# The bias of V passed through Wo once, in place of a bias matmul in every V product

## The chip, the core and the metric

One Trainium2 chip; the program runs on one of its cores. The time is device microseconds (us) of one execution, and each kernel's figure is the median of its runs. Names of engines: PE is the matrix engine (TensorE), DVE VectorE, ACT ScalarE, POOL GpSimd, and SP the engine whose queue issues the DMAs here (SyncE).

## The reference

A gated block for eight batch items of 512 rows by 512 columns: cross attention with 16 heads of 32 columns, and then a feed-forward part with ternary weights. Cut to what the change touches:

```python
V = _linear(value, Wv, bv)                 # value @ Wv.T + bv, value is ctx_1024, 512 x 512 for each item
attn = jax.nn.softmax(qk / (2.0 * t), axis=-1)
out = jnp.einsum('bhqk,bhkd->bhqd', attn, V)
out = out.transpose(0, 2, 1, 3).reshape(b, sq, d)
return _linear(out, Wo, bo)                # out @ Wo.T + bo
...
x = x + jnp.tanh(g_xattn[0]) * _L0_xattn_ref(_layernorm(x), ctx_1024, ctx_1024, ...)
x = x + jnp.tanh(g_ffn[0]) * _L0_ffn_ref(_layernorm(x), w1, w2)
```

The rows of `attn` sum to one, so the bias `bv` reaches `out` unchanged in every row, and Wo turns it into one vector that is the same for all items: `Wo @ bv`. That vector and `bo` are added to the same result. What is computed besides: a temperature t for each head, from statistics of the scores and of their softmax (stage A below), a layer norm of x ahead of Q, and a quantisation of the activations in the feed-forward part.

## The kernel before

**Products.** Every f32 operand of Q, K, V and Wo is split into two f16 parts, high and low. One product of a 128x512 tile is twelve matmuls (four chunks of the contraction, and for each high x high, high x low, low x high), summed in one PSUM bank, by `split_product`. A bias is a thirteenth matmul: ones (128x128) times `bias16`, a tile that is zero except for two rows, the high and the low part of the bias (L1432 in `split_product`). K and Q get their biases on ACT as they leave PSUM; V and the Wo product (called W) get them by the thirteenth matmul.

**Stages.** `body(i)` runs on each engine for i = -1, 0, then three turns of a loop of two bodies for i = 1 to 6, then 7 and 8. In one body three things are interleaved: stage A of item i (64 score tiles, each a matmul L1455, a row maximum on DVE L998, an exponential on ACT L778, statistics on DVE L1008), stage B of item i-1 (its real attention, then W, the residual, the norm and the feed-forward part), and stage P of item i+1 (products K, V, Q, and the turned x). For i = -1 there is only P of the first item, for i = 0 no B, for 7 no P.

**Order within a body**, the same on all engines and written out by hand: 16 sets of stage B with 40 of the 64 A tiles among them; then the products K0 to K3, W0 to W3, the turned x, V0 to V2, Q0, Q1, the four transposes of the quantised residual (`turned_xq`, L1592), Q2, Q3, with the remaining A tiles spread over them by `A_PLAN`; then the feed-forward part (`up`, `turn`, `down`), and V3 after `up(1)`. Each engine runs its instructions in program order and waits on semaphores. Four PSUM banks (b_ps twice, o_ps, z_ps) are used in turn for all products (`mm_use`, `take`, by the list of uses in `bank_uses`); `take` makes PE wait until the bank's last user has drained it. In i = 0, eight chunks of the feed-forward weights are made ternary besides: their magnitudes are summed first (ACT L768 and DVE L1290), and chunk 7 is the last to be loaded.

**The first item's setup.** SP issues all loads in one row: Wk, ctx, x, Wq, then the small vectors (`bq` and `bk` laid out with one element for each partition and group, L561 and L562; the gates L563 and L564; `bv` and `bo` as rows copied to all partitions, L565 and L566), Wv, Wo, the small weights and three feed-forward chunks; then `stack` (the K and Q parts laid out for the scores, L493, L480, L487, 12 DMAs each), which waits for the splits of K and Q on POOL (L684). ACT runs a tanh of the two gates (L752) ahead of its first product drain (L847 and L851).

Of the kernel before, what the change touches and what calls it, by code (L numbers as in the profile page):

```python
# [72 lines left out]
BIAS_STEPS = 5  # L73
# [6 lines left out]
FIRST_V_AT = {1: 2, 3: 3}  # L80
POOL_CHUNKS, DVE_CHUNKS = (3, 2), (0, 1, 6, 7, 4, 5)
# [48 lines left out]
def bank_uses(setup, has_p, has_b, has_a):  # L130

    def some(stage, count, present=True):
        return [(stage, k) for k in range(count)] if present else []

    uses = some("S", 2, setup == 0) + some("K", C, has_p) + some("W", T, has_b)
    if setup == 0:
        uses += some("V", T, has_p) + some("X", T, has_p)
    else:
        uses += some("X", T, has_p) + some("V", T - 1, has_p and setup is None)
    uses += some("Q", C, has_p)[:2] + some("xq", T, has_b and has_p) + some("Q", C, has_p)[2:]  # L140
    uses += some("V", T, has_p and setup == -1)
# [82 lines left out]
def flamingo_kernel(nc, x, ctxT, g_xattn, g_ffn, WqT, bq, WkT, bk, WvT, bv, WoT, bo,  # L224
                    w1T, b1, w2T, b2, w3T, b3, f1T, f2T, out):
    with ExitStack() as ctx:
# [59 lines left out]
        bias16 = sb("bias16", [P, 2, D], F16)  # L286
        bias_row = vbuf[0][:, 0:2, :]
        bias_hi = vbuf[0][:, 2, :].bitcast(F16).rearrange("p (k n) -> p k n", k=2)
# [70 lines left out]
        bias_in, bias_step = sem("bias_in"), sem("bias_step")  # L359
# [76 lines left out]
        def _(sp):  # L436
# [149 lines left out]
        def _(pool):  # L586
# [21 lines left out]
            pool.memset(bias16[:, :, :], 0.0).then_inc(bias_step, 1)  # L608
# [67 lines left out]
            def body(i, par):  # L676
# [30 lines left out]
                for n in range(C):  # L707
                    if has_p:
                        split_qk(n)
                    if second and n % 2 == 1:  # L710
                        normalise_x(1, n // 2, from_cin)
                        split_x(1, n - 1, from_cin)
                        split_x(1, n, from_cin)
                    if has_b and n == 1:
                        split_y(i - 1, C - 1)
                if second:
                    make_ternary(3)
# [257 lines left out]
        def _(dve):  # L975
# [281 lines left out]
            def make_ternary(n):  # L1257
# [17 lines left out]
            vec.tensor_copy(bias16[0:1, :, :], bias_hi[0:1, :, :]).then_inc(bias_step, 1)  # L1275
            vec.scalar_tensor_tensor(out=bias16[DK:DK + 1, :, :], in0=bias_row[DK:DK + 1, :, :], scalar=WSCALE,
                                     in1=bias_hi[DK:DK + 1, :, :], op0=ALU.mult, op1=ALU.subtract) \
                .then_inc(bias_step, 1)
            weight_lo(2, "v")
# [13 lines left out]
            def body(i, par):  # L1293
                has_a, has_b, has_p = stages(i)
                second = isinstance(i, int) and i == 0
                for s in range(SETS):
# [5 lines left out]
                    if has_p and has_b and s in X_STATS_AT:  # L1302
                        stat_x(i + 1, X_STATS_AT.index(s))
                    if second and s in SUMS_AT:
                        ternary_sum(SUMS_AT[s])
# [97 lines left out]
        def _(pe):  # L1403
# [14 lines left out]
            def split_product(bank_n, left, right, tiles=(), bias=None):  # L1418
# [7 lines left out]
                for n, (c, l, r) in enumerate(pairs):  # L1426
                    if n in places:
                        places[n]()
                    ins = mat(mm_ps[bank_n][:, :], left[l](c), right[r](c),  # L1429
                              start=(c, l, r) == pairs[0], stop=bias is None and (c, l, r) == pairs[-1])  # L1430
                if bias is not None:
                    ins = mat(mm_ps[bank_n][:, :], ones16[:, :], bias16[:, bias, :], start=False, stop=True)  # L1432
# [56 lines left out]
            def body(i, par):  # L1489
# [41 lines left out]
                def w_part(t, chunks):  # L1531
# [5 lines left out]
                    if chunks[-1] == C - 1:  # L1537
                        mat(mm_ps[bank_n][:, :], ones16[:, :], bias16[:, 1, :], start=False, stop=True) \
# [18 lines left out]
                for t in range(T) if has_p or not has_b else ():  # L1557
                    if has_b:
                        split_product(take(i, "W", t),
                                      [lambda c, l=l: yT[:, l, c, t * P:(t + 1) * P] for l in range(2)],  # L1560
                                      [lambda c, w=w: w["o"][:, c, :] for w in (w_hi, w_lo)], tiles_a(C + t), bias=1)
# [12 lines left out]
                def v_products(tiles_of=range(T)):  # L1574
                    for t in tiles_of:
# [37 lines left out]
                for n in range(C):  # L1613
# [7 lines left out]
                    if first and n == C - 1:  # L1621
                        pe_waits.wait_ge(w_lo_done, 3)
                        pe_waits.wait_ge(bias_step, BIAS_STEPS)
                        v_products()
                    if has_b and has_p and n == 1:
# [139 lines left out]
```

## Time and profile before

| | |
|---|---|
| median of three runs | 1337.31 us (1337.2 to 1338.84) |
| the profiled execution, its own time | 1338.21 us |
| its span in the trace | 1336.3 us |
| PE busy | 89% |
| DVE busy | 82% |
| ACT busy | 70% |
| granted clock of PE, mean over the span | 0.967 |

Busy time is the sum of an engine's instructions; for PE their ends are modelled and the instructions overlap, so a busy PE is not one at its peak. The chain of work that ended last is followed back from the last instruction, at each step to what released it. Where two releasers are nearly as late as each other, it names only one of them. Times of rows are counted from the start of the span.

### The profile page before, as it was taken

To read this page: it belongs to the slowest core of one execution; us is meant where nothing else is said; L and a number is where in the kernel's file an instruction comes from. 1 tells how busy PE (TensorE), PEld (TensorE's weight loads), DVE (VectorE), ACT (ScalarE), POOL (GpSimd) and SP (SyncE) were. 2 spreads that over 40 slices of the span, in tenths; PEclk is the share of its full clock that TensorE was granted. 3 is DMA by queue.
4 is the path that set the end of the run, shared out by engine and by line. 5 is a ranking of instruction groups with operands and counts; after the bars stand their busy time and mean duration, and the time that the engine had idled before them with its cause. 6 is when DMAs were issued, how large, how long until landed. Compare 5 with 4: busy or idle time off the path is not lost.

```text
span 1336.3 us, 23530 instructions
## 1 busy us (share of the span) xinstructions
PE 1183.3 (89%) x6684; PEld 438.0 (33%) x6684; DVE 1097.7 (82%) x2054; ACT 936.5 (70%) x1568; POOL 394.2 (29%) x387
## 2 busy tenths in 40 slices
PE   4856598989999999998999999998989899859988
PEld 2322221444124421444124432344214441224234
DVE  7789789896998869896998869897898979985256
ACT  4676599565985679575985669665885669765833
POOL 3148555311452024510353124510353101200120
PEclk9878789999999999999999999999999999979989
DMA  8712211221112221211112221112212210001000
GB/s 311 233 58 64 48 48 49 48 48 57 33 41 48 57 74 49 48 36 39 54 49 48 51 79 48 25 25 65 64 49 49 48 65 1 1 1 42 23 0 32
DMA packets 36049, 73.70 MB, mean 55 GB/s; under 512 B 8144, under 2 KB 8528, under 8 KB 35408
## 3 DMA queue, kind: packets, MB, share of 16 engines
q1 hardware_dynamic: 35920, 72.13, 18.9%
q8 instruction: 62, 1.02, 0.3%
q14 instruction: 67, 0.55, 0.1%
HBM read 38.39 MB, written 8.39 MB: 35 GB/s over the span
## 4 chain that ended last, share of the span: by engine, by line
PE 50%; DVE 26%; issue 10%; ACT 8%; SPq 3%; DMA 1%; DVEq 1%; POOL 1%; ACTq 0%; POOLq 0%
PE b_ps L1429 10%; DVE stat L1008 7%; PE o_ps L1669 6%; DVE nmax L998 5%; PE o_ps L1474 4%; PE o_ps L1429 4%; PE b_ps L1461 4%; ACT region L810 4%; PE a_ps L1455 4%; PE z_ps L1429 4%; ACT etile L778 3%; DVE hmax L1204 2%; PE z_ps L1669 2%; PE z_ps L1485 2%; PE b_ps L1634 2%
## 5 line engine op out<-in xcount | busy, mean ns | idle before, releaser
L778 ACT ACTIVATE etile<-a_ps,nmax 128x512 f32<-128x512 f32 x512 | 368.0, 732 | 113.8 <-DVE nmax L998 113.5
L810 ACT ACTIVATE region<-b_ps,inv2t 128x512 f32<-128x512 f32 x512 | 353.2, 754 | 49.9 <-PE b_ps L1461 45.8
L998 DVE TENSOR_REDUCE nmax<-a_ps 128x1 f32<-128x512 f32 x512 | 345.5, 677 | 51.7 <-PE a_ps L1455 48.1
L1008 DVE BATCH_NORM_STATS2 stat<-etile 128x6 f32<-128x512 f32 x500 | 339.8, 682 | 16.0 <-ACT etile L778 15.7
L1455 PE MATMUL a_ps<-kst,qst 96*128 96x512 f16 x512 | 198.8, 392 | 32.9 <-ACT etile L778 26.7
L1461 PE MATMUL b_ps<-qst,kst 97*128 97x512 f16 x512 | 193.0, 389 | 22.4 <-DVE region L1230 7.8
L1474 PE MATMUL o_ps<-region,vbuf 128*32 128x512 f32 x1024 | 137.3, 608 | 10.7 <-ACT region L810 7.0
L1485 PE MATMUL z_ps<-region,ones 128*32 128x512 f32 x1024 | 136.2, 604 | 9.5 <-DVE region L1040 9.5
L1461 PEld LDWEIGHTS b_ps<-qst,kst 97*128 97x128 f16 x512 | 49.3, 96 | 288.9 <-ACT region L810 258.1
L684 POOL TENSOR_TENSOR region<-region 128x512 f16<-128x512 f32 x64 | 77.0, 1203 | 210.9 <-ACT region L851 210.9
L640 POOL TENSOR_TENSOR region<-region 128x512 f32<-128x512 f32 x32 | 40.8, 1276 | 288.9 <-DVE region L1047 288.9
L1204 DVE TENSOR_REDUCE hmax<-region 128x1 f32<-128x512 f32 x128 | 82.1, 680 | 13.2 <-ACT region L931 12.1
L613 POOL CAST c_hi<-cin 128x512 f16<-128x512 f32 x28 | 17.1, 610 | 243.8 <-DMA cin<-in_ctxT_dram 243.3
L1669 PE MATMUL o_ps<-f,region 128*128 128x512 fp8e4 x352 | 79.6, 379 | 0.0
L1455 PEld LDWEIGHTS a_ps<-kst,qst 96*128 96x128 f16 x512 | 50.9, 99 | 82.4 <-ACT etile L778 45.3
L1634 PE MATMUL b_ps<-f,region 128*128 128x512 fp8e4 x256 | 62.9, 383 | 14.2 <-DVE region L1230 11.5
L931 ACT ACTIVATE region<-b_ps,xmax 128x512 f32<-128x512 f32 x64 | 43.4, 689 | 26.3 <-PE b_ps L1634 26.0
L661 POOL TENSOR_SCALAR cin<-cin,mv,rstd 128x512 f32<-128x512 f32 x28 | 58.0, 2077 | 2.8 <-POOL rstd L652 2.6
L941 ACT ACTIVATE region<-b_ps 128x1024 f16<-128x1024 f16 x31 | 31.7, 1023 | 31.8 <-PE b_ps L1645 31.0
L1037 DVE TENSOR_SCALAR region<-o_ps 128x512 f32<-128x512 f32 x32 | 21.7, 680 | 37.0 <-PE o_ps L1474 37.0
L650 POOL TENSOR_SCALAR rstd<-mv 128x2 f32<-128x2 f32 (+1 forms) x25 | 5.8, 231 | 137.6 <-DVE mv L1353 52.4
L1669 PEld LDWEIGHTS o_ps<-f,region 128*128 128x128 f16 x352 | 33.7, 98 | 38.1 <-issue 1.0
(312 smaller groups left out, 1977.8 us busy)
## 6 DMA issues: line engine op xcount, KB each, us to landing
kst<-region SPq DMA_DIRECT2D x96, 128.0 KB, 2.3
qst<-region SPq DMA_DIRECT2D x84, 128.0 KB, 2.3
xres<-in_x_dram SPq DMA_DIRECT2D x8, 1024.0 KB, 5.5
out_dram<-xres SPq DMA_DIRECT2D x32, 256.0 KB, 2.0
cin<-in_ctxT_dram SPq DMA_DIRECT2D x30, 256.0 KB, 2.7
cin<-in_x_dram SPq DMA_DIRECT2D x28, 256.0 KB, 2.6
kst<-in_f1T_dram SPq DMA_DIRECT2D x2, 1024.0 KB, 9.4
qst<-in_f2T_dram SPq DMA_DIRECT2D x2, 1024.0 KB, 9.0
```

Source lines behind the costliest of these rows:

```text
L778: nc.scalar.activation(etile[:, k % E_SLOTS, :], a_ps[k % A_BANKS][:, :], ACT.Exp, bias=nmax[:, slot_of(n), t:t + 1], scale=1.0, accum_out ...
L810: nc.scalar.activation(probs[:, (s + 1) % 2, g, :], b_ps[g % 2][:, :], ACT.Exp, scale=inv2t[:, slot:slot + 1]).then_inc(b_exp, 1)
L998: vec.tensor_reduce(nmax[:, slot_of(k // T), k % T:k % T + 1], a_ps[k % A_BANKS][:, :], AX.X, ALU.max, negate=True).then_inc(a_max, 1)
L1008: vec.bn_stats(stat[:, slot_of(k // T) * T + k % T, :], etile[:, k % E_SLOTS, :]).then_inc(a_stat, covered)
L1204: ins = vec.tensor_reduce(hmax[:, n:n + 1], hbuf[t % 2][:, n * S:(n + 1) * S], AX.X, ALU.max, apply_absolute_value=True)
L1429: ins = mat(mm_ps[bank_n][:, :], left[l](c), right[r](c), start=(c, l, r) == pairs[0], stop=bias is None and (c, l, r) == pairs[-1])
L1455: mat(a_ps[k % A_BANKS][:, :], qst[par][0:SHIFT, slot, t * P:(t + 1) * P], kst[par][0:SHIFT, slot, :], start=True, stop=True).then_inc(a_f ...
L1461: mat(b_ps[g % 2][:, :], kst[par][0:SHIFT + 1, slot, k * P:(k + 1) * P], qst[par][0:SHIFT + 1, slot, :], start=True, stop=True).then_inc(b ...
L1474: ins = mat(o_ps[g * DK:(g + 1) * DK, :], vbuf[par][:, k, n * DK:(n + 1) * DK], probs[:, (s + 1) % 2, g, :], start=k == 0, stop=k == T - 1)
L1485: ins = mat(z_ps[g * DK:(g + 1) * DK, :], ones32[:, 0:DK], probs[:, (s + 1) % 2, g, :], start=k == 0, stop=k == T - 1)
L1634: ins = mat(mm_ps[bank_n][:, :], xqT[:, c, t * P:(t + 1) * P], f1[:, c, n * S:(n + 1) * S], start=c == 0, stop=c == C - 1)
L1669: ins = mat(mm_ps[bank_n][:, :], hT[t % 2][:, k, :], f2[:, k, :], start=k == 0, stop=k == KC - 1)
```

## The change

The thirteenth matmul of the V products is left out. In the setup of the first item `Wo @ bv` is computed once: SP loads `bv` into `bvc` with one element for each partition and chunk (as `bq` is loaded); POOL splits it into two f16 parts and spreads each over 64 columns (`spread_bv`); PE runs a product of twelve matmuls and the bias matmul of `bo`, 64 partitions wide, as a new use "O" of a PSUM bank behind V3 (`bias_product`); DVE takes it from PSUM behind set 13 of i = 0 and writes its high and low parts into `bias16` (`join_biases`), which now has one bias in place of two.

```diff
+BIAS_AT = 13
@@ bank_uses
-    uses += some("V", T, has_p and setup == -1)
+    uses += some("V", T, has_p and setup == -1) + some("O", 1, setup == -1)
@@ SP, setup
                 sp.dma_start(bqk[:, 1, :], bk.rearrange("(g p) -> p g", p=P)).then_inc(bqk_in, 16)
+                sp.dma_start(bvc[:, :], bv.rearrange("(g p) -> p g", p=P)).then_inc(bias_in, 16)
             sp.dma_start(gates[:, 0:1], g_xattn.partition_broadcast(P)).then_inc(gate_in, 16)
             sp.dma_start(gates[:, 1:2], g_ffn.partition_broadcast(P)).then_inc(gate_in, 16)
-            sp.dma_start(bias_row[:, 0, :], bv.partition_broadcast(P)).then_inc(bias_in, 16)
-            sp.dma_start(bias_row[:, 1, :], bo.partition_broadcast(P)).then_inc(bias_in, 16)
+            sp.dma_start(bias_row, bo.partition_broadcast(P)).then_inc(bias_in, 16)
@@ POOL; called in body(-1) behind the splits of K
+            def spread_bv():
+                pool_waits.wait_ge(bias_in, 32)
+                pool.tensor_copy(bv_parts[:, 0, :], bvc[:, :]).then_inc(bv_step, 1)
+                pool_waits.wait_ge(bv_step, 1)
+                pool.tensor_tensor(bv_parts[:, 1, :], bvc[:, :], bv_parts[:, 0, :], ALU.subtract).then_inc(bv_step, 1)
+                pool_waits.wait_ge(bv_step, 2)
+                pool.tensor_copy(bv_wide[:, :, :], bv_parts[:, :, :].rearrange("p l c -> p (l c)").unsqueeze(2)
+                                 .broadcast_to([P, 2 * C, HALF])).then_inc(bv_step, 1)
@@ DVE; called in body(0) behind set 13
+            def join_biases():
+                bank_n, before = mm_use(-1, "O")
+                dve_waits.wait_ge(mm_full[bank_n], before + 1)
+                vec.tensor_copy(bias_sum[0:HALF, :], mm_ps[bank_n][0:HALF, :]).then_inc(bias_step, 1)
+                dve_waits.wait_ge(bias_step, BIAS_STEPS + 1)
+                vec.tensor_copy(bias16[0:1, :], bias_sum[0:1, :]).then_inc(bias_step, 1)
+                vec.tensor_tensor(bias16[DK:DK + 1, :], mm_ps[bank_n][DK:DK + 1, :], bias_sum[DK:DK + 1, :],
+                                  ALU.subtract).then_inc(mm_free[bank_n], 1)
@@ PE, v_products
-                                          tiles_a(C + T + t) if t < T - 1 or not has_b else (), bias=0)
+                                          tiles_a(C + T + t) if t < T - 1 or not has_b else ())
@@ PE; called in body(-1) behind v_products
+                def bias_product():
+                    bank_n = take(i, "O")
+                    pe_waits.wait_ge(bv_step, 3)
+                    pe_waits.wait_ge(w_lo_done, 4)
+                    for n, (c, l, r) in enumerate((c, l, r) for c in range(C) for l, r in ((0, 0), (0, 1), (1, 0))):
+                        mat(mm_ps[bank_n][0:HALF, :], bv_wide[:, l * C + c, :], (w_hi, w_lo)[r]["o"][:, c, :],
+                            start=n == 0, stop=False)
+                    mat(mm_ps[bank_n][0:HALF, :], ones16[:, 0:HALF], bias16[:, :], start=False, stop=True) \
+                        .then_inc(mm_full[bank_n], 1)
```

What this moves in the engines' orders, at three places. On PE, at the end of the first item's setup, the last three matmuls of V3 (wv, c) are followed by the bias matmul and then by the A tiles of i = 0 (kst, qst). Before:

```order
L1429 MATMUL b_ps<-wv_hi,c_hi 128x512
L1429 MATMUL b_ps<-wv_lo,c_hi 128x512
L1429 MATMUL b_ps<-wv_hi,c_lo 128x512
L1432 MATMUL b_ps<-bias,ones 128x512
L1455 MATMUL a_ps<-kst,qst 128x512 x8
```

And in the changed kernel:

```order
L1460 MATMUL b_ps<-wv_hi,c_lo 128x512
L1624 MATMUL b_ps<-wo_hi,bv_wide 64x512
L1624 MATMUL b_ps<-wo_lo,bv_wide 64x512
L1624 MATMUL b_ps<-wo_hi,bv_wide 64x512 x2
L1624 MATMUL b_ps<-wo_lo,bv_wide 64x512
L1624 MATMUL b_ps<-wo_hi,bv_wide 64x512 x2
L1624 MATMUL b_ps<-wo_lo,bv_wide 64x512
L1624 MATMUL b_ps<-wo_hi,bv_wide 64x512 x2
L1624 MATMUL b_ps<-wo_lo,bv_wide 64x512
L1624 MATMUL b_ps<-wo_hi,bv_wide 64x512
L1626 MATMUL b_ps<-bias,ones 64x512
L1486 MATMUL a_ps<-kst,qst 128x512 x8
```

The bias matmul of V3 is gone, and thirteen narrower ones stand ahead of the A tiles (the first two pairs of A tiles stand ahead of V2 and V3 in both kernels).

On DVE, in i = 0, the row maximum and the statistics of set 13 are followed by those of set 14. In the changed kernel:

```order
L1016 TENSOR_REDUCE nmax<-a_ps 128x1
L1026 BN_STATS stat<-etile 128x6
L1302 CAST bv_wide<-b_ps 64x512
L1304 COPY bias<-bv_wide 1x512
L1305 TENSOR_TENSOR bias<-b_ps,bv_wide 1x512
L1016 TENSOR_REDUCE nmax<-a_ps 128x1
L1026 BN_STATS stat<-etile 128x6
L1260 TENSOR_REDUCE wsum<-wabs 128x1
```

The three rows in the middle are new; the rows around them stand next to each other in the kernel before (as L998, L1008 and L1242).

On SP, in the setup, the small vectors stood before the change as

```order
L562 DMA bqk<-in_bk_dram 128x4x1
L563 DMA gates<-in_g_xattn_dram 128x1
L564 DMA gates<-in_g_ffn_dram 128x1
L565 DMA vbuf<-in_bv_dram 128x512
L566 DMA vbuf<-in_bo_dram 128x512
L551 DMA xres<-in_WvT_dram 128x4x512
```

and stand now as

```order
L567 DMA bqk<-in_bk_dram 128x4x1
L568 DMA bvc<-in_bv_dram 128x4x1
L569 DMA gates<-in_g_xattn_dram 128x1
L570 DMA gates<-in_g_ffn_dram 128x1
L571 DMA vbuf<-in_bo_dram 128x512
L556 DMA xres<-in_WvT_dram 128x4x512
```

The load of bv has moved ahead of the two gates and has the form of the loads of bq and bk.

## Rows read from the trace of the kernel before

**Rows 1.** The page: busy time (share) of two engines, and the chain by engine.
```profile
PE 1183.3 (89%) x6684; PEld 438.0 (33%) x6684; DVE 1097.7 (82%) x2054; ACT 936.5 (70%) x1568; POOL 394.2 (29%) x387
...
PE 50%; DVE 26%; issue 10%; ACT 8%; SPq 3%; DMA 1%; DVEq 1%; POOL 1%; ACTq 0%; POOLq 0%
```

**Rows 2.** The chain in time, at V0 of i = 1: start us, us, what.
```profile
260.36 2.59 PE b_ps L1429 x12
262.96 0.22 PE b_ps L1432
263.17 0.22 PE a_ps L1455
```

**Rows 3.** Waits over the whole span: us in total, times, longest us.
```profile
PEld b_ps L1592 <- ACT region L851: 6.2, 6, 1.0
```

**Rows 4.** Timeline of i = 1 around Q1, ACT, then PE: start us, us, [idle before <- releaser].
```profile
273.53 0.69 ACT L778 ACTIVATE etile<-a_ps,nmax 128x512 f32<-128x512 f32 x1 [0.50 <-DVE nmax L998]
...
275.35 1.27 ACT L778 ACTIVATE etile<-a_ps,nmax 128x512 f32<-128x512 f32 x2
276.52 0.69 ACT L847 ACTIVATE region<-b_ps,bqk 128x512 f32<-128x512 f32 x1
...
277.93 0.40 PE L1592 MATMUL b_ps<-ident,region 128*128 128x128 f16 x4 [0.86 <-ACT region L851]
```

**Rows 5.** Windows: length, busy us (x instructions) of each engine, PE clock, DMA share.
```profile
262.50:277.90 15.40, 13.84 (x73) 6.32 (x70) 15.14 (x29) 9.36 (x19) 1.16 (x1) 1.00 0.01 2
...
74.60:129.40 54.80, 39.90 (x156) 14.78 (x156) 54.69 (x82) 37.76 (x53) 33.73 (x27) 0.84 0.19 48
```

**Rows 6.** Timeline of PE in i = 1, from the end of V3 on.
```profile
294.05 0.38 PE L1432 MATMUL z_ps<-bias,ones 128*128 128x512 f16 x1
294.61 1.07 PE L1645 MATMUL b_ps<-ident,region 128*128 128x128 f16 x16 [0.18 <-DVE region L1221]
```

**Rows 7.** Timeline of SP's DMA issues in the setup.
```profile
6.73 4.23 SPq L563 DMA_DIRECT2D gates<-in_g_xattn_dram  x1
...
22.33 1.59 SPq L474 DMA_DIRECT2D kst<-ones  x1
30.08 8.45 SPq L493 DMA_DIRECT2D kst<-region  x12
...
48.76 7.60 SPq L487 DMA_DIRECT2D qst<-region  x12
...
58.63 1.07 SPq L514 DMA_DIRECT2D region<-in_f2T_dram  x1
```

**Rows 8.** Timeline of the setup: ACT's tanh of the gates, POOL's splits of K and Q.
```profile
18.17 0.20 ACT L752 ACTIVATE tg<-gates 128x2 f32<-128x2 f32 x1 [1.76 <-DMA gates<-in_g_ffn_dram]
...
22.40 1.54 POOL L684 TENSOR_TENSOR region<-region 128x512 f16<-128x512 f32 x1 [0.82 <-ACT region L851]
24.99 1.31 POOL L684 TENSOR_TENSOR region<-region 128x512 f16<-128x512 f32 x1 [1.05 <-ACT region L851]
27.58 2.48 POOL L684 TENSOR_TENSOR region<-region 128x512 f16<-128x512 f32 x1 [1.28 <-ACT region L851]
37.22 1.20 POOL L684 TENSOR_TENSOR region<-region 128x512 f16<-128x512 f32 x1 [7.17 <-ACT region L851]
```

**Rows 9.** Timeline of i = 0's first sets: PE, ACT, DVE.
```profile
55.34 1.05 PE L1455 MATMUL a_ps<-kst,qst 96*128 96x512 f16 x3
...
70.10 1.91 ACT L768 ACTIVATE f<-region 128x2048 f32<-128x2048 f32 x1 [2.81 <-DMA region<-in_f2T_dram]
...
72.71 0.69 DVE L1008 BATCH_NORM_STATS2 stat<-etile 128x6 f32<-128x512 f32 x1 [2.50 <-ACT etile L778]
...
74.60 2.65 DVE L1262 SCALAR_TENSOR_TENSOR f<-kst,whalf,f 128x2048 fp8e4<-128x2048 f32 x1 [1.14 <-ACT f L759]
```

**Rows 10.** Nearest operations to the join's three: page (us, mean ns), then timeline.
```profile
L1037 DVE TENSOR_SCALAR region<-o_ps 128x512 f32<-128x512 f32 x32 | 21.7, 680 | 37.0 <-PE o_ps L1474 37.0
...
30.71 0.41 DVE L1275 COPY bias<-vbuf 1x1024 f16<-1x1024 f16 x1
```

More of the change, by code:

```diff
@@ L72 @@
 LOWEST = -3.0e38
-BIAS_STEPS = 5
+BIAS_STEPS, HALF = 5, 64
 SETUP_STEPS = G4 + 6
@@ L285, in flamingo_kernel @@
         ones16 = sb("ones16", [P, P], F16)
-        bias16 = sb("bias16", [P, 2, D], F16)
-        bias_row = vbuf[0][:, 0:2, :]
-        bias_hi = vbuf[0][:, 2, :].bitcast(F16).rearrange("p (k n) -> p k n", k=2)
+        bias16 = sb("bias16", [P, D], F16)
+        bv_wide = sb("bv_wide", [P, 2 * C, HALF], F16)
+        bv_parts = sb("bv_parts", [P, 2, C], F16)
+        bvc = sb("bvc", [P, C])
+        bias_row = vbuf[0][:, 0, :]
+        bias_hi = vbuf[0][:, 2, :].bitcast(F16)[:, 0:D]
+        bias_sum = bv_wide[:, :, :].rearrange("p k n -> p (k n)")
         bqk = sb("bqk", [P, 2, C])
@@ L358, in flamingo_kernel @@
         bq_scaled = sem("bq_scaled")
-        bias_in, bias_step = sem("bias_in"), sem("bias_step")
+        bias_in, bias_step, bv_step = sem("bias_in"), sem("bias_step"), sem("bv_step")
         mm_full = [sem(f"mm_full{n}") for n in range(MM)]
@@ L607, in _ @@
             pool.memset(ones16[:, :], 1.0).then_inc(bias_step, 1)
-            pool.memset(bias16[:, :, :], 0.0).then_inc(bias_step, 1)
+            pool.memset(bias16[:, :], 0.0).then_inc(bias_step, 1)
+            def spread_bv():
[6 more added lines that the diff above has]
+                                 .broadcast_to([P, 2 * C, HALF])).then_inc(bv_step, 1)
             def split_c(b, c):
@@ L715, in body @@
                         split_y(i - 1, C - 1)
+                if first:
+                    spread_bv()
                 if second:
@@ L1274, in _ @@
             dve_waits.wait_ge(bias_step, 3)
-            vec.tensor_copy(bias16[0:1, :, :], bias_hi[0:1, :, :]).then_inc(bias_step, 1)
-            vec.scalar_tensor_tensor(out=bias16[DK:DK + 1, :, :], in0=bias_row[DK:DK + 1, :, :], scalar=WSCALE,
-                                     in1=bias_hi[DK:DK + 1, :, :], op0=ALU.mult, op1=ALU.subtract) \
+            vec.tensor_copy(bias16[0:1, :], bias_hi[0:1, :]).then_inc(bias_step, 1)
+            vec.scalar_tensor_tensor(out=bias16[DK:DK + 1, :], in0=bias_row[DK:DK + 1, :], scalar=WSCALE,
+                                     in1=bias_hi[DK:DK + 1, :], op0=ALU.mult, op1=ALU.subtract) \
                 .then_inc(bias_step, 1)
+            def join_biases():
[6 more added lines that the diff above has]
+                                  ALU.subtract).then_inc(mm_free[bank_n], 1)
             weight_lo(2, "v")
@@ L1303, in body @@
                         stat_x(i + 1, X_STATS_AT.index(s))
+                    if second and s == BIAS_AT:
+                        join_biases()
                     if second and s in SUMS_AT:
@@ L1416, in drained, with split_product @@
                 pe_waits.wait_ge(mm_free[bank_n], before + 1)
-            def split_product(bank_n, left, right, tiles=(), bias=None):
+            def split_product(bank_n, left, right, tiles=(), bias=False):
                 tiles = list(tiles)
@@ L1429, in split_product @@
                     ins = mat(mm_ps[bank_n][:, :], left[l](c), right[r](c),
-                              start=(c, l, r) == pairs[0], stop=bias is None and (c, l, r) == pairs[-1])
-                if bias is not None:
-                    ins = mat(mm_ps[bank_n][:, :], ones16[:, :], bias16[:, bias, :], start=False, stop=True)
+                              start=(c, l, r) == pairs[0], stop=not bias and (c, l, r) == pairs[-1])
+                if bias:
+                    ins = mat(mm_ps[bank_n][:, :], ones16[:, :], bias16[:, :], start=False, stop=True)
                 ins.then_inc(mm_full[bank_n], 1)
@@ L1537, in w_part @@
                     if chunks[-1] == C - 1:
-                        mat(mm_ps[bank_n][:, :], ones16[:, :], bias16[:, 1, :], start=False, stop=True) \
+                        mat(mm_ps[bank_n][:, :], ones16[:, :], bias16[:, :], start=False, stop=True) \
                             .then_inc(mm_full[bank_n], 1)
@@ L1560, in body @@
                                       [lambda c, l=l: yT[:, l, c, t * P:(t + 1) * P] for l in range(2)],
-                                      [lambda c, w=w: w["o"][:, c, :] for w in (w_hi, w_lo)], tiles_a(C + t), bias=1)
+                                      [lambda c, w=w: w["o"][:, c, :] for w in (w_hi, w_lo)], tiles_a(C + t), bias=True)
                     else:
@@ L1624, in body @@
                         v_products()
+                        bias_product()
                     if has_b and has_p and n == 1:
```

## The prediction, made before the changed kernel ran

> **What bounds the kernel now.** I read the page first. PE is the busiest engine, 1183.3 us or 89% of a span of 1336.3 us, and half of the chain that ended last lies on it [rows 1]. Taken alone this says that a matmul less is time less. The share is a mean over stages, though, so I went on to the place where the matmuls are removed: the chain in order of time through one middle item, i = 1. There it runs straight through the V products: twelve matmuls in 2.59 us, the bias matmul 0.22 us, one A tile 0.22 us [rows 2]. That gives the price of a 512-column matmul at the full clock: 2.59 / 12 = 0.216 us.
>
> The chain names one releaser where two are nearly tied, so the next thing to look for is a wait of PE soon after V that another engine ends. It is there. The fourth transpose of the quantised residual needs the PSUM bank of Q1, and PE stands for it until ACT has drained Q1: the wait is in the list six times, 6.2 us in total, never over 1.0 us, once for each of the six middle items [rows 3]. In i = 1 the transpose starts at 277.93 after 0.86 us of idle matmul time [rows 4]. So the question is what sets ACT's drain. ACT starts it at 276.52; before it ACT runs two exponentials from 275.35 on without a gap, before them the drain of Q0, and before that an exponential at 273.53 that had waited 0.50 us for a row maximum of DVE [rows 4]. And DVE is full: 15.14 us of the 15.40 us from 262.50 to 277.90 [rows 5] are instructions, the rest are the short steps between chained ones. Its work in this stretch (the norm and the quantisation of the residual, and the row maxima and statistics of the A tiles) starts from the last W product, which PE issues ahead of the V products. From W3 to 277.9 the stage is therefore set by DVE and then ACT, and PE arrives early. What the V products save lies wholly inside.
>
> **Removed: 32 matmuls.** Eight items with four V products each, at 0.216 us, are 6.9 us of PE time. By place:
>
> - V0 to V2 of the six middle items: 18 matmuls, 3.9 us. They move Q0 and Q1 by 0.65 us per item, and then PE waits 0.65 us longer for ACT's drain. Worth 0. A Q1 that is ready 0.65 us earlier cannot start ACT's drain earlier, because ACT is in the exponentials until 276.5 either way.
> - V3 of the six middle items: 6 matmuls, 1.3 us. Its bias matmul starts at 294.05 and takes 0.22 us, to 294.27; the turned hidden tile behind it starts at 294.61 and has waited for DVE's quantisation, 0.18 us of it idle [rows 6]. Worth 0; the wait becomes about 0.4 us.
> - The four V products of i = 0 (for the second item): DVE is busy 54.69 us of the 54.80 us from 74.60 to 129.40, PE 39.90 us [rows 5]. Worth 0.
> - The four of the setup: 0.86 us on PE ahead of the A tiles. They are taken together with what is added there.
>
> **Added on PE: the product O**, thirteen matmuls 64 wide. No such matmul stands in the trace. The moving side has 512 columns as in V, so I take 0.216 us each, 2.8 us; the lower bound is nothing, the upper one twice that at the lower clock, 5.6 us. The fifth and later A tiles stand behind V3, at 55.34 [rows 9]; they come at 55.34 - 0.86 + 2.81 = 57.3, 1.95 us later. What waits for them are DVE's row maxima and ACT's exponentials. But both engines come to a stop later anyway: ACT stands 2.81 us, until 70.10, for chunk 7 of the feed-forward weights, and DVE 2.50 us behind that [rows 9]. 1.95 us fits into 2.81 us, so the price is 0; at the upper bound the tiles come 4.7 us late and 1.9 us stand over. Three A tiles right there take 1.05 us together [rows 9], less than three at twice 0.216 us, so I keep to the full clock. If that DMA landed earlier by more than 0.9 us, the difference would begin to show.
>
> What sets that landing is SP: it issues the 12 + 12 + 4 + 12 + 2 DMAs from 30.08 to 58.6 practically without a gap, the first of them released by POOL's last split of K at 27.58 + 2.48 = 30.06, and then chunk 7 at 58.63 [rows 7, 8]. This row of issues is the true chain of the first 70 us, and nothing in the change shortens it.
>
> **Added on DVE: the join**, three instructions behind set 13 of i = 0. Nearest rows: a 128x512 read from PSUM 0.68 us, a one-row copy 0.41 us [rows 10]. Bounds: 3 x 0.41 = 1.2 us and 3 x 0.68 = 2.0 us; I take 0.68 + 0.41 + 0.68 = 1.8 us. At this place DVE has 2.50 us of waiting ahead of it and 1.14 us more ahead of 74.60 [rows 9], 3.64 us in all. The A tiles come late by up to 1.95 us, the join takes 1.8 us: 3.75 us. That is a tie within 0.1 us, and at the upper bounds (2.0 + 1.95) 0.3 us over. I price it at 0, with +0.3 us as the other end. DVE's setup instructions on the bias become half as wide; they lie ahead of the Wv split, which waits for ACT, and are worth 0.
>
> **Added on POOL**: two instructions on 128x4 and a spread of 128x512, behind the K splits. Even at three times the longest split, 7.4 us [rows 8], they all but fit into the 7.17 us that POOL then stands idle; I expect 1 to 3 us. Worth 0.
>
> **Added on SP: the load of bv by elements**, 512 of 4 bytes, ahead of the gates, for a row copy of 256 KB less behind them. This is the unknown. Right behind the two loads of this form SP needed 4.23 us for one small issue, that of the first gate [rows 7]. ACT then stood 1.76 us, to 18.17, for the second gate, and its first drain of K is behind that [rows 8]. Bounds for the delay d of the gates: 0, and once more the 4.23 us. Behind it stand ACT's drains and POOL's splits; POOL's splits of K1, K2, K3 were each preceded by idle time, 0.82 + 1.05 + 1.28 = 3.15 us [rows 8]. Only the part of d above 3.15 us reaches the split at 27.58, and with it SP's row of issues: 0 at the lower end, 4.23 - 3.15 = 1.1 us at the upper one. SP itself has 30.08 - 23.92 = 6.2 us to spare there [rows 7]. Two earlier loads together went with 4.23 us, one more should add less: d of 1 to 2 us, price 0.
>
> The Trainium skill, page "DMA: Bandwidth & Descriptors", section "Rules for kernel authors", advises against this form: a non-contiguous last dimension becomes one descriptor per element. It gives no time for 512 of them, and the trace agrees as far as the 4.23 us do; the bounds above stand without it.
>
> **Sum.** 0 from the V products, 0 from O (up to +1.9) and the join (up to +0.3), 0 from POOL, 0 from SP (up to +1.1). The profiled execution took 1338.21 us for its span of 1336.3; it would take the same, and the median of the runs, 0.9 us below it, stays as well: **1337.3 us**. PE's busy time does fall, by 19 matmuls.
>
> **Rivals.** All are told against 0.2%, 2.7 us, which is about what a measurement of this kernel can tell from no change.
>
> 1. *The chain is right and PE bounds the items.* Then every matmul counts: 19 x 0.216 = 4.1 us, 1333.2 us. For it: the chain passes through all V products [rows 2]. Against: the wait at the transposes in all six items [rows 3], and a DVE without a gap [rows 5]. Chance 0.07. The Trainium skill, page "TensorE: Matmul & The Clock Gate", section "Back-to-back issue gap", gives about 131 ns per 512-column matmul in a stream with weight loads; by that the rival would be worth 2.5 us, 1334.8 us. The rows say 216 ns.
> 2. *The load by elements costs far more than its elders.* The gates land d later; ACT's tanh, the K drains, POOL's K3 split and SP's row of 42 issues move by d - 3.15 us, and all items with them. It decides (over 2.7 us) from d = 5.85 us on; with d = 8.5 us, twice the stall that the trace shows, the time would be 1337.3 + 5.3 = 1342.6 us. For it: a single stall of 4.23 us is already there. Against: the bound above. Chance 0.08.
> 3. *The first item's waits do not cover O and the join.* Uncovered they are 1.95 + 1.8 = 3.75 us, 1341.1 us. It decides when less than 1.05 us of the 3.64 us is still there, for instance with chunk 7 landing early. Against: the landing hangs on SP alone. Chance 0.05.
>
> **How the numbers follow.** The forecast of no change has 0.80. Its own spread is about that of the runs shown, 1.6 us, and the upper ends of the sum, 0.3 + 1.1 + 1.9 = 3.3 us, reach to 1340.6; below, the spread and a part of the V products' 4.1 us reach to 1335.0. The range 1335.0 to 1340.6 leaves out the first rival and about half of what the others give, some 0.15. Faster by over 0.2%: 0.07; within it: 0.80; slower: 0.08 + 0.05 = 0.13.
>
> **What would show it.** In the changed trace: the idle time of PE ahead of the fourth transpose, 0.86 us now, at about 1.5 us; the one ahead of the turned hidden tile at about 0.4 us; each item as long as before; chunk 7 issued near 58.6 and landed near 70.1; ACT's wait for it down from 2.8 us to about 1 us; the join between 70 and 73 us; the tanh at 18.2 plus d. The prediction is wrong if items become shorter (DVE was not the bound behind W3), or if the K3 split on POOL starts later than 27.6 us.

## The result, and the profile after

The changed kernel took 1343.92 us in the median (1342.01 to 1347.28, 10 runs) against 1338.94 us (1337.2 to 1344.54, 10 runs) of the kernel before: a ratio of 1.0038 with a 95% interval of 1.0023 to 1.0053. It is slower by 0.4%, outside the range that I gave. The profiled execution took 1343.54 us, its span 1341.4 us.

The page of the changed kernel, busy time and the chain by engine, beside [rows 1]:

```profile
PE 1186.8 (88%) x6665; PEld 438.1 (33%) x6665; DVE 1099.9 (82%) x2057; ACT 936.8 (70%) x1568; POOL 393.7 (29%) x390
...
PE 44%; DVE 31%; issue 11%; ACT 8%; POOL 1%; DVEq 1%; SPq 1%; ACTq 0%; DMA 0%; POOLq 0%
```

PE has 19 matmuls less, as counted, and 3.5 us *more* busy time. Fewer instructions with more time in them point to a lower clock somewhere, and are the first hint that the loss isn't at the place of the change.

The timeline of PE in i = 1 (start us, us, what, idle before and its releaser) at the two places where my steps on V looked, beside [rows 4] and [rows 6]:

```profile
276.54 0.40 PE L1634 MATMUL b_ps<-ident,region 128*128 128x128 f16 x4 [1.49 <-ACT region L869]
...
293.40 1.06 PE L1688 MATMUL b_ps<-ident,region 128*128 128x128 f16 x16 [0.57 <-DVE region L1239]
```

Both waits grew by what the bias matmuls had taken: 0.86 to 1.49 us and 0.18 to 0.57 us. Here nothing was gained, as forecast.

The setup and i = 0's first sets, from the timeline of each engine (SP, ACT, POOL, PE, DVE), beside [rows 7 to 9]:

```profile
6.58 4.38 SPq L568 DMA_DIRECT2D bvc<-in_bv_dram  x1
11.01 1.37 SPq L569 DMA_DIRECT2D gates<-in_g_xattn_dram  x1
...
58.68 1.35 SPq L519 DMA_DIRECT2D region<-in_f2T_dram  x1
...
16.48 0.19 ACT L770 ACTIVATE tg<-gates 128x2 f32<-128x2 f32 x1
...
70.07 1.91 ACT L786 ACTIVATE f<-region 128x2048 f32<-128x2048 f32 x1 [0.23 <-DMA region<-in_f2T_dram]
...
28.24 1.75 POOL L700 TENSOR_TENSOR region<-region 128x512 f16<-128x512 f32 x1 [1.42 <-ACT region L869]
...
30.78 1.06 POOL L622 COPY bv_wide<-bv_parts 128x512 f16<-128x512 f16 x1
...
58.29 1.04 PE L1486 MATMUL a_ps<-kst,qst 96*128 96x512 f16 x4
...
58.72 0.69 DVE L1016 TENSOR_REDUCE nmax<-a_ps 128x1 f32<-128x512 f32 x1 [3.57 <-PE a_ps L1486]
...
72.08 0.67 DVE L1302 CAST bv_wide<-b_ps 64x512 f16<-64x512 f32 x1
72.78 0.28 DVE L1304 COPY bias<-bv_wide 1x512 f16<-1x512 f16 x1
73.09 0.68 DVE L1305 TENSOR_TENSOR bias<-b_ps,bv_wide 1x512 f16<-1x512 f32 x1
...
75.20 2.34 DVE L1280 SCALAR_TENSOR_TENSOR f<-kst,whalf,f 128x2048 fp8e4<-128x2048 f32 x1
```

The 4.4 us stall of SP is there once, not twice: the load by elements of bv has taken it from the first gate. The tanh came at 16.48, not behind 18.17. POOL's K3 split started at 28.24, later than the 27.6 that I had named as a sign of being wrong, but it was shorter: it ended at 29.99, against 30.06 before, and chunk 7 was issued at 58.68, against 58.63. The fifth A tile came at 58.29 (55.34 before), the join took 1.7 us, and the next large instruction of DVE ends at 75.20 + 2.34 = 77.54, against 74.60 + 2.65 = 77.25: 0.3 us late. So all that the change adds cost 0.3 us at this place.

**Where the time went.** The row maximum that opens an item, in the changed kernel's timeline of DVE, and the same row of the kernel before:

```profile
624.53 1.29 DVE L1016 TENSOR_REDUCE nmax<-a_ps 128x1 f32<-128x512 f32 x2
...
780.64 1.29 DVE L1016 TENSOR_REDUCE nmax<-a_ps 128x1 f32<-128x512 f32 x2
```

```profile
625.03 1.29 DVE L998 TENSOR_REDUCE nmax<-a_ps 128x1 f32<-128x512 f32 x2
...
778.21 1.29 DVE L998 TENSOR_REDUCE nmax<-a_ps 128x1 f32<-128x512 f32 x2
```

Until half way the changed kernel is 0.5 us *ahead*. One item later it is 2.4 us behind: 156.1 us for the item in place of 153.2. The windows of the changed kernel at two places of that item (length, busy us and instructions of each engine, PE clock, DMA share):

```profile
664.00:667.60 3.60, 1.82 (x15) 0.37 (x11) 2.89 (x9) 2.54 (x5) 2.32 (x3) 0.97 0.01 2
667.60:671.00 3.40, 3.40 (x16) 0.53 (x13) 3.37 (x6) 2.42 (x4) 3.32 (x3) 0.53 0.00 0
...
763.00:767.00 4.00, 4.00 (x23) 2.30 (x21) 3.32 (x8) 1.30 (x3) 0.00 (x0) 0.58 0.02 4
```

The granted clock fell to its half, 1.2 GHz, twice, from 667.4 and from 763.0, and twice again one turn of the loop later, from 978.0 and from 1073.6 (the first expectation below has these times 0.2 us later). In the kernel before's profile it does not fall at all between 175 and 1178 us. Neither place has anything to do with V: ahead of the second, PE stands 1.63 us for DVE in both kernels, and ahead of the first nearly the same 1.8 us. The timeline of PE in the changed kernel, then in the kernel before, and the window of the kernel before that follows:

```profile
666.62 1.24 PE L1516 MATMUL z_ps<-region,ones 128*32 128x512 f32 x8 [1.78 <-DVE region L1058]
```

```profile
667.13 1.07 PE L1485 MATMUL z_ps<-region,ones 128*32 128x512 f32 x8 [1.77 <-DVE region L1040]
...
667.00:670.40 3.40, 3.19 (x21) 0.70 (x21) 3.17 (x9) 1.92 (x4) 3.40 (x2) 1.00 0.00 0
```

The same pause is followed by half clock in one execution and not in the other. That was a cause that I hadn't priced, but it isn't the only one, as the experiments showed.

### The profile page after: what moved, and what is told of

Read it like the earlier page. It is cut to its first block, busy times and chain, and to the rows that moved or that the text cites. A ratio compares the mean times of both kernels' runs of the same rounds, so it can differ in the third digit from the quotient of the medians.

```text
span 1341.4 us, 23497 instructions
## 1 busy us (share of the span) xinstructions
PE 1186.8 (88%) x6665; PEld 438.1 (33%) x6665; DVE 1099.9 (82%) x2057; ACT 936.8 (70%) x1568; POOL 393.7 (29%) x390
## 4 chain that ended last, share of the span: by engine, by line
PE 44%; DVE 31%; issue 11%; ACT 8%; POOL 1%; DVEq 1%; SPq 1%; ACTq 0%; DMA 0%; POOLq 0%
DVE stat L1026 8%; PE b_ps L1460 7%; DVE nmax L1016 6%; PE o_ps L1712 6%; PE o_ps L1505 5%; PE b_ps L1492 4%; ACT region L828 4%; PE a_ps L1486 3%; PE o_ps L1460 3%; ACT etile L796 3%; PE z_ps L1460 3%; PE z_ps L1516 2%; DVE hmax L1222 2%; PE z_ps L1712 2%; PE b_ps L1677 2%
## 5 line engine op out<-in xcount | busy, mean ns | idle before, releaser
L1505 PE MATMUL o_ps<-region,vbuf 128*32 128x512 f32 x1024 | 140.4, 612 | 12.3 <-ACT region L828 7.0
```

The lines of the kernel that those rows point to most:

```text
L1505: ins = mat(o_ps[g * DK:(g + 1) * DK, :], vbuf[par][:, k, n * DK:(n + 1) * DK], probs[:, (s + 1) % 2, g, :], start=k == 0, stop=k == T - 1)
```

## The experiments

All ratios are to the kernel before on the same chip, with 95% intervals. The median of the kernel before was 1338.61 us beside runs 1 to 4, 1340.90 beside 5 to 7, 1339.17 beside 8 to 11, 1339.94 beside 12 to 15.

### Which half of the change? (runs 1 to 4)

**e1**, the kernel before, and **e2**, the changed kernel, unedited.

> The kernel before, once more, for its own spread and a second trace. Theory G (clock gate): the 5 us lie in the middle items, where the changed kernel's trace shows four stretches at half clock (667.6, 763.2, 978.2 and 1073.8 us) and the first trace of before shows none between 174.7 and 1178 us; which executions have such stretches varies, so some executions of before should have them as well and be 2 to 6 us longer, with a lower mean clock. Theory S (setup): before stays without them, 1337 to 1340 us.

> The changed kernel once more. Theory G: the time follows the mean clock from execution to execution, some executions without any half-clock stretch in the middle items and then within 1 us of before. Theory S: 1.0038 of before in each, whatever the clock.

Measured: 0.9993 (0.9981 to 1.0006) and 1.0037 (1.0025 to 1.0049). The loss is real. e1 ran from 1334.97 us at a mean clock of 0.969 to 1343.44 us at 0.963, as theory G had it; but the shortest execution of e2 took 1341.73 us, and G had expected some within 1 us of the kernel before. The clock alone doesn't carry the loss.

**e3**, the kernel before without V's thirteenth matmul; V's bias is missing from the result, and the setup is untouched:

```diff
-     tiles_a(C + T + t) if t < T - 1 or not has_b else (), bias=0)
+     tiles_a(C + T + t) if t < T - 1 or not has_b else ())
```

> Only the removal: the kernel before without the thirteenth matmul of the V products (the bias of V is left out of the result), its setup untouched. Theory V (the thinner V products make the gate fall in the middle items): slower than before by 0.2 to 0.4%, with half-clock stretches there. Theory S (the setup's changes shift the items against the gate, or cost by themselves): as before within 0.1%.

**e4**, the changed kernel with a thirteenth matmul in V again (it adds `bias16`, a wrong bias for V, at the old cost):

```diff
-     tiles_a(C + T + t) if t < T - 1 or not has_b else ())
+     tiles_a(C + T + t) if t < T - 1 or not has_b else (), bias=True)
```

> Only the addition: the changed kernel with a thirteenth matmul put back into each V product (it adds the wrong bias to V, so the result is not the reference's). Theory V: as fast as before within 0.1%. Theory S: slower than before by 0.2 to 0.5%, as the changed kernel.

Measured: e3 0.9992 (0.9980 to 1.0003), e4 1.0004 (0.9993 to 1.0016). Neither half alone is slower, so each of the theories V and S has one half right and the other wrong. With them falls any theory in which the work of each half has a price and the two prices add up: with each half at nothing, their sum had to be nothing.

What was left was to follow DVE's instructions in e2 and e4 one by one through each item. They drift apart at few places, and two of them, behind 481 and behind 790 us, have no half clock. There PE stands in "issue", waiting for nothing that the profile shows, in the middle of a set of eight value matmuls. The timeline of PE, changed kernel, at the first place:

```profile
477.40 0.60 PE L1492 MATMUL b_ps<-qst,kst 97*128 97x512 f16 x2
478.41 1.04 PE L1505 MATMUL o_ps<-region,vbuf 128*32 128x512 f32 x2 [0.41 <-DVE xres L1254]
479.97 1.06 PE L1505 MATMUL o_ps<-region,vbuf 128*32 128x512 f32 x6 [0.51 <-issue]
480.96 0.39 PE L1492 MATMUL b_ps<-qst,kst 97*128 97x512 f16 x1
```

The kernel before has such a pause too, but a little further on, behind the eighth:

```profile
479.27 1.07 PE L1474 MATMUL o_ps<-region,vbuf 128*32 128x512 f32 x8 [0.18 <-DVE xres L1236]
481.58 0.39 PE L1461 MATMUL b_ps<-qst,kst 97*128 97x512 f16 x1 [1.24 <-issue]
```

In e3 it comes still later, within the next set, and e4 has none:

```profile
480.06 2.07 PE L1485 MATMUL z_ps<-region,ones 128*32 128x512 f32 x8
```

```profile
478.62 1.06 PE L1505 MATMUL o_ps<-region,vbuf 128*32 128x512 f32 x8
479.62 0.39 PE L1492 MATMUL b_ps<-qst,kst 97*128 97x512 f16 x1
```

Both places are the first instructions of the loop's body, when `Fori(0, 3)` turns back (it holds two items a turn: 1 and 2, 3 and 4, 5 and 6). And there the queue that loads instructions is busy. The DMA view of the kernel before from 430 to 450 us, then from 470 to 490 (packets, MB, share):

```profile
q8 instruction: 1, 0.02, 0.3%
...
q8 instruction: 3, 0.05, 1.1%
```

Three loads of 16 KB in 20 us, where in the 20 us from 430 on there is one. They start at 475.5, 479.1 and 483.9, and PE goes on 2.5 us behind the second. In the changed kernel they start at 474.6, 477.8 and 483.3, and PE goes on 2.2 us behind the second.

Counted in the built programs, with two instructions for each matmul that the trace shows (weight load and matmul), the loop's head stands 11 instructions later in the changed kernel (26 for product O and 1 for a wait, less 16 for eight bias matmuls of V ahead of the loop), 16 earlier in e3, 27 later in e4. The pause comes behind 25 instructions from the head in the kernel before, 14 in the changed one, 41 to 42 in e3. 25 - 11 = 14, and 25 + 16 = 41: **the pause stays where it is in PE's code, and the change shifts the loop across it**. For e4, 25 - 27 is less than nothing: the head lies beyond that place.

### Shift the code, change no work (runs 5 to 7)

The edit stands ahead of PE's first instruction, where PE has nothing to do for 13.6 us. Two such waits become one instruction:

```diff
             pe_waits = Waits(pe, stood)
+            for _ in range(64):
+                pe.wait_ge(ident_in, 1)
```

64 waits in the changed kernel are 32 instructions (e5); 86 in the kernel before are 43 (e6), and 22 are 11 (e7).

> The changed kernel with 32 PE instructions more ahead of its first matmul, each a wait on two semaphore counts that stand long before (PE has nothing to do for its first 13 us), so that the loop over pairs of batches begins 32 instructions later in PE's code; no work differs. Theory L (code loading): at each of the two turns back to the loop's head PE runs dry for 0.5 to 2 us, in the changed kernel after the first 2 of 8 value matmuls of item 3 and of item 5, in the kernel before 11 instructions further on, in the run without V's bias matmul 16 further on than that, always at the same place of the code counted from PE's start, and in the changed kernel with the thirteenth matmul back the loop's head lies past that place and nothing is lost. L expects no such pause behind the loop's head, items 3 and 5 at 153.0 to 153.6 us, and a median of 1338.5 to 1340.5 us. Theory C (clock): the V products leave PE emptier, so that TensorE falls to half clock more often; the shift changes nothing and the median is 1343 to 1344 us.

> The kernel before with 43 such PE instructions more ahead of its first matmul, which puts its loop's head at the same place of PE's code as in e5. Theory L expects the pauses of 1.24 and 1.38 us at 481.58 and 789.11 to be gone, items 3 and 5 at about 153.2 us in place of 154.2 and 154.5, and a median 2 to 3 us under the kernel before, 1335.6 to 1336.6 us. Theory C expects the median of the kernel before, 1338.6 us within 0.8. Between e5 and e6 only the change itself is left, with no pause at the turns in either: L expects e5 to be 2 to 4 us longer, from the clock and the setup.

> The kernel before with 11 such PE instructions more, which puts its loop's head where the changed kernel has it; no work differs from before. Theory L expects the pause after the first 2 of 8 value matmuls behind the loop's head, as in the changed kernel, of 1.0 to 2.0 us, items 3 and 5 at 154.5 to 155.5 us, and a median of 1339 to 1340.5 us, 0.5 to 2 over the kernel before. Theory C expects 1338.6 us within 0.8 and the pause where it was.

Measured: e5 1339.70 us, 0.9994 (0.9983 to 1.0004), items 3 and 5 at 153.2 us both. e6 1338.56 us, 0.9981 (0.9969 to 0.9992), items 3 and 5 at 153.3 and 153.0. e7 1342.16 us, 1.0008 (0.9998 to 1.0019), items 3 and 5 at 155.3 and 154.9; its two pauses are 1.27 and 0.89 us. PE at the first turn, in e5:

```profile
478.90 1.06 PE L1507 MATMUL o_ps<-region,vbuf 128*32 128x512 f32 x8
479.89 0.39 PE L1494 MATMUL b_ps<-qst,kst 97*128 97x512 f16 x1
```

and in e7, whose work is that of the kernel before:

```profile
477.42 1.04 PE L1476 MATMUL o_ps<-region,vbuf 128*32 128x512 f32 x2
479.73 1.06 PE L1476 MATMUL o_ps<-region,vbuf 128*32 128x512 f32 x6 [1.27 <-issue]
```

Thirty-two instructions that do nothing took the changed kernel's loss away; theory C falls, and theory L is shown in its main point. (e5 ran on another chip than e2; e11 below is the same comparison on one chip.) Against the kernel before on their chip e6 and e7 differ by -2.3 and +1.3 us, as L had it, though the interval of e7 just takes in no change. The times in us that I had named for the two were too low: that chip's kernel before stood at 1340.90, not 1338.61. And L missed once: it had expected e5 to be 2 to 4 us longer than e6, and the difference is 1.1 us. One thing more is in e7: its profile falls to half clock at 666.8, 762.4, 977.4 and 1073.0, the changed kernel's at 667.4, 763.0, 978.0 and 1073.6. So these four stretches don't need the change either.

### All on one chip, and the length of a piece (runs 8 to 11)

e8 is the changed kernel, e9 that of e7, e11 that of e5. e10 is the changed kernel shifted by 245 instructions, so that its head stands 256 behind that of the kernel before.

> The changed kernel once more, beside the next three on one chip and against the kernel before. Place alone explains it (theory L): the same time as the kernel before shifted by 11 (second run below) plus what the change costs at an equal place, 1.1 us by the two shifted kernels e5 and e6: a ratio of 1.0025 to 1.0040. If the change and the place act on each other (theory LC: the pause and the emptier V products together bring more half-clock stretches in the middle items than each alone), the ratio is over the sum of the two, 1.0035 or more.

> The kernel before with its loop's head where the changed kernel has it, once more. L: the larger part of the changed kernel's loss, 1.0015 to 1.0030. LC: a small part of it, about 1.0008 as in e7.

> The changed kernel with 245 PE instructions more ahead of its first matmul, which with its own 11 makes 256 more than the kernel before has. If code comes in pieces of 16 KB (62 loads, 1.02 MB in the page's row of the queue) of 256 instructions, the loop's head stands in its piece as in the kernel before, and L expects the pause behind 8 value matmuls, ahead of the next score, of 0.9 to 1.4 us, and before + 1 to 2 us, a ratio of 1.0008 to 1.0018. If the pieces are not what sets the place, the pause stays or goes elsewhere. PE's first matmul must still come at 13.6 us, else the waits themselves cost.

> The changed kernel shifted by 32 once more, on the same chip as the unshifted one. L: 0.0025 to 0.0045 under it, and within 0.1% of the kernel before.

Measured: e8 1343.37 us, 1.0037 (1.0023 to 1.0051); e9 1342.29 us, 1.0026 (1.0014 to 1.0039); e11 1339.61 us, 1.0005 (0.9993 to 1.0017). The place alone gives e9 about two thirds of the loss, more than the quarter in e7 (1.0008), and the shift by 32 takes 3.8 us from the changed kernel. The two theories aren't told apart by e8: its 1.0037 lies in the range of both.

e10 took 1356.89 us, 1.0139 (1.0121 to 1.0158), far from what I expected, and its profile says why: 245 instructions of waiting are not hidden by 13.6 us. PE's first matmul (first row) came 17.3 us late. What is left without them is 1339.6 us. But the pause stood where the theory had put it, behind the eighth value matmul as in the kernel before:

```profile
30.90 0.59 PE L1462 MATMUL b_ps<-c_hi,wk_hi 128*128 128x512 f16 x1 [30.90 <-issue]
...
497.71 1.06 PE L1507 MATMUL o_ps<-region,vbuf 128*32 128x512 f32 x8 [0.36 <-DVE xres L1254]
500.20 0.39 PE L1494 MATMUL b_ps<-qst,kst 97*128 97x512 f16 x1 [1.42 <-issue]
```

So the pattern repeats after 256 instructions. That this is one load of 16 KB fits the size of the loads.

### What is left at an equal place (runs 12 to 15)

e12 is e6 again, e15 is e5 again. e13 is e3 shifted by 59 and e14 is e4 shifted by 16, each with the head at the same place as the other two; what they leave out of the result or get wrong in it is what e3 and e4 do.

> First of four kernels whose loop's head stands at the same place of PE's code, with no pause behind it; they differ in the two halves of the change alone. This one has neither half. Theory L from e6: 0.9981 of the kernel before, within 0.0012.

> Second of the four: only V's bias matmul is gone (V's bias is left out of the result), nothing is added in the setup. My prediction's steps on V (worth 0): the same as e12 within 0.5 us. Theory V, in which the emptier V products cost time of their own: 1 us or more over e12.

> Third of the four: the gather, the O product and the join are there, and V's thirteenth matmul too (so the bias that reaches V is wrong). My prediction's steps on the setup: 0 to 0.5 us over e12. Theory S, in which the setup costs what the changed kernel loses at equal place: 1 us or more over e12.

> Last of the four: both halves, the changed kernel shifted by 32. 1.1 us over e12, as e5 was over e6 and e8 over e9, if that difference is more than chance.

Measured: e12 1338.09 us, 0.9988 (0.9974 to 1.0002); e13 1339.79, 0.9992 (0.9978 to 1.0006); e14 1339.75, 1.0001 (0.9988 to 1.0014); e15 1339.57, 1.0000 (0.9985 to 1.0015). At an equal place the changed kernel is 1.1, 1.1 and 1.5 us longer (e5 over e6, e8 over e9, e15 over e12). My prediction's steps had put e13 within 0.5 us of e12 and e14 at 0 to 0.5 us over it; measured are 1.7 us over e12 for both, and 1.5 us for both halves together. Each of the four ratios has an interval of about 1.9 us on each side, so these differences bear out neither the steps nor the theories V and S: the runs can't assign the 1.1 to 1.5 us, nor tell them from chance, and I leave them open.

**The price of the pause**, over all seventeen profiles: the time from the first value matmul behind the loop's head to the next score, at the two turns back.

| head's place (instructions against before) | kernels | us, at each turn | over 1.00 |
|---|---|---|---|
| -16 | e3 | 1.00, 1.00 (the pause is a set later: 1.0 and 0.5 us) | |
| 0 (or +256) | before, e1, e10 | 2.31, 2.45; 1.95, 2.20; 2.49, 2.14 | mean 1.26 |
| +11 | changed, e2, e8, e7, e9 | 2.55, 2.83; 3.05, 3.59; 3.31, 3.07; 3.31, 2.92; 2.97, 3.72 | mean 2.13 |
| +27, +43 | e4 and e14, e5, e6, e11 to e13, e15 | 1.00 in all sixteen | 0 |

Two turns cost 2.5 us at the place of the kernel before and 4.3 us at that of the changed one. The second of the three loads seems to start when PE comes to the loop's head (at 479.1 in the kernel before and 477.8 in the changed one, 0.6 and 0.4 us behind the start of the body's first scores), and PE goes on 2.2 to 2.8 us behind its start, in the sixteen turns of the two middle rows; at +11 six value matmuls and the score are still behind it, at 0 the score alone. The differences of medians fit the table: before to its unpaused version -2.3 (e6) and -1.9 us (e12), where 2.5 is due; the changed kernel to its own -3.8 us (e8 to e11), where 4.3 is due. Kernels without a pause have three close loads too (e6 from 470 to 490 us, and e5 from 473.2 to 478.8); what differs is only whether PE stands for one of them.

The fastest version that the runs have is the kernel before with 43 idle instructions ahead (e6, e12): 0.9981 and 0.9988, the second with an interval that just takes in 1. The changed kernel with the same cure only reaches the time of the kernel before.

## Why the prediction was wrong

The forecast was no change at 1337.3 us, with 1335.0 to 1340.6; measured was +5.0 us. By its own steps:

- **V0 to V2, worth 0: right.** The wait at the fourth transpose was to be 1.5 us and is 1.49; the next item is no sooner. **V3, worth 0: right**; the wait was to be 0.4 and is 0.57 us. Rival 1, PE as the bound, is out: in e3, which has the removal of all 32 matmuls and nothing else, it would give 6.9 us less, 0.9948, and the interval ends at 0.9980; e13 isn't faster than e12 either.
- **Product O, 2.8 us, price 0: right, with one term off.** It took 55.36 to 58.29, 2.9 us. The 0.86 us that I had taken off ahead of it did not show: the V products started 0.80 us later (at 44.04, against 43.24) and so ended no sooner than before. Their delay comes from the first K product, whose matmuls stood 0.43 us apart, twice the 0.216 us, until 18.7 in place of 17.5; that is scatter, for in the profiles of the changed kernel they start from 42.31 (e15) to 44.35 us (e8), and in those of the kernel before from 43.24 to 45.22 (e9). So the fifth A tile came 2.95 us late, not 1.95, and ACT's wait for chunk 7 shrank from 2.81 to 0.23 us (I had said about 1). The cover was thinner than I thought, and it held.
- **The join, 1.8 us and a tie: right.** 0.67 + 0.28 + 0.68 us, 1.7 us with the gaps, 0.3 us at the end, which is the upper bound that I gave. It ended at 73.77, a little behind the 73 that I had named. Rival 3 is out with it.
- **The load of bv, 0 to 1.1 us: right in the price, wrong in the sign of d.** The stall did not add up, and the tanh came 1.7 us earlier, where I had said 1 to 2 us later. The K3 split started 0.66 us later all the same, since ACT's first drain, at 18.38 before, now stood until 18.99 for PE's slower first K product; by its end it released SP's row at 30.01 (30.08 before). Rival 2 is out. **POOL, 1 to 3 us: right**, 29.94 to 31.84, hidden.
- **The sum: this is the step that failed.** It reads "0 from the V products, 0 from O ..." and takes for granted that what isn't edited keeps its time. I costed instructions by the engine time of their work, and not by the room that they take in PE's code, so the wait of PE at each turn of the loop had no term at all. The 11 instructions that the change adds on balance ahead of the loop put the load of the next piece behind the second value matmul instead of the eighth, 0.87 us more at each of two turns: 1.7 us of the 5.0. e7 and e9 show the place alone at +1.3 and +3.1 us.
- **No term for the granted clock.** The profile of before had no half clock in its middle items, the one of after four stretches. e4 has one alone, at 761 us: its item took 154.9 us in place of 153.2, 1.7 us. The one at 978 us cost the changed kernel 1.1 us, by the row maxima of DVE against e4's. Twice both are 5.6 us, so in this one profiled pair the clock is nearly the whole difference. The runs don't bear that out as the rule: the fourteen profiles outside place 0 have between one and four such stretches in the middle items, also where there is no pause (e11, e12, e13, e15: three). Over all their executions the mean granted clock is 0.9662 for e2 and e8 and 0.9677 for the kernel before beside them (0.9652 for the changed kernel's first ten, beside which the kernel before has none on record), and a stretch such as that from 667.4 to 670.8 is 3.4 x 0.5 / 1340 = 0.0013 of it: about one stretch more, 1.1 to 1.7 us. The 120 executions of the kernel before beside the experiments give the exchange rate: in each batch, 0.001 less of mean clock goes with 0.8 us more (a straight line through them, within 0.14). The 0.0015 are 1.2 us by it. But one batch of the kernel before (beside e5 to e7) has a mean of 0.9662 itself, so a difference of this size comes and goes without any change. The pauses' 1.7 us and the 1.1 to 1.5 us at equal place leave 1.8 to 2.2 us of the 5.0. That this rest is the clock is argued from those means, not shown, and it is no larger than the intervals of the terms.

Of "what would show it", the two waits behind V and chunk 7 at 58.7 and 70.1 came in as told. ACT's wait, the end of the join, the tanh and the K3 split were off as said, at no cost. And items had to keep their length: items 4 and 6 didn't (156.1 and 155.9 us), at places that the change doesn't touch.

The evidence was in the trace of before: 1.24 us ahead of a score that nothing releases, once in each of two turns. In the view of waits it stands among PE's own pace (total us, times, longest us), for the weight loads of values and scores, before:

```profile
PEld o_ps L1474 <- issue: 31.1, 95, 1.0
...
PEld b_ps L1461 <- issue: 14.9, 13, 2.3
```

and in the changed kernel:

```profile
PEld o_ps L1505 <- issue: 35.2, 97, 1.7
...
PEld b_ps L1492 <- issue: 13.6, 14, 1.4
```

The totals say little; the longest has moved from the score (2.3) to the values (1.7).

## What to carry over

In a kernel whose loop body is some thousands of instructions long, an edit ahead of the loop or in it moves the place at which the engine runs dry at each turn; before a small loss or gain is put down to the edit's work, shift the code by a few idle instructions and measure both kernels at an equal place. An "issue" wait of about a microsecond in the middle of like instructions just behind the turn of a loop, with loads on the instruction queue near it, is the mark; three close loads by themselves are not, since the kernels without a pause have them too. And an edit that saves time under a wait has no gain to set against such accidents, so it isn't safe even where each of its steps is free.

## What I hadn't expected of the hardware

- Code comes on queue 8 in loads of 16 KB, 62 of them in the span of the kernel before, and the pattern of PE's pause repeats after 256 instructions (e10). The Trainium skill, page "Advanced Engine Details and Errata", section "ISA Cache", has cache lines of 16 KB for 256 instructions, and only two of them. The runs agree on the first. The same section gives TensorE 128 KB where it gives 32 KB otherwise, which is more than two such lines; how many PE keeps, no run here shows.
- A pause at the turn of the loop that costs 0.9 to 2.7 us by the place of the loop's head (0.5 and 1.0 us a set later in e3), and none at all at +27 and +43 instructions.
- 245 idle instructions at PE's start, each two waits on counts long reached, brought its first matmul from 13.6 to 30.90 us; 43 of them moved it by less than 0.1 us.
- One load by elements of 512 x 4 bytes more behind two of its kind moved SP's stall of 4.23 us to itself (4.38 us) and didn't lengthen it.
